# Eight heads' expert weights: added on GpSimd and transposed once, in place of four accumulating products on TensorE

## The chip, the core and the metric

The kernel runs on one core of a Trainium2 chip. The metric is the device time of one execution in microseconds (us). A core has five instruction queues that run side by side and meet only through semaphores: TensorE (PE in the rows, its weight loads PEld), VectorE (DVE), ScalarE (ACT), GpSimd (POOL) and SyncE (SP), which here only issues transfers.

## What is computed

A layer norm, an attention block with three branches (compressed, selected, windowed), and a feed-forward part that picks experts by product keys; the output is x + attention * silu(feed-forward). The change lies in the feed-forward part:

```python
q = (x @ Wq.T).reshape(b, n, 2, HEADS, DIM_KEY).transpose(2, 0, 1, 3, 4)
sim = jnp.einsum('pbnhd,hkpd->pbnhk', q, keys)
sx, ix = jax.lax.top_k(sim[0], TOPK)          # HEADS = 8, TOPK = 16
sy, iy = jax.lax.top_k(sim[1], TOPK)
all_scores = (sx[..., :, None] + sy[..., None, :]).reshape(b, n, HEADS, TOPK * TOPK)
scores, pk_indices = jax.lax.top_k(all_scores, TOPK)
wd = W_down[pk_indices]
wu = W_up[pk_indices]
h = jnp.einsum('bnd,bnhkd->bnhk', x, wd)
h = jax.nn.gelu(h, approximate=False)
h = h * jax.nn.softmax(scores, axis=-1)
return jnp.einsum('bnhk,bnhkd->bnd', h, wu)
```

The indices are places in the 16x16 grid of rank pairs, the same grid for all heads, and only 50 of its places can be among the first 16. So for each token the kernel needs, for each of these 50 experts, the softmax weight summed over the eight heads. It then multiplies that sum by the gelu of the expert's product and multiplies the result by the matrix of experts.

## The kernel before

The input has 8 batches of 512 tokens, cut into 32 tiles of 128 tokens (TILES; four to a batch, TB). All five programs are written out by hand, as `turn(n)` for n = 0 to 31, with a ring of buffers between them. A tile passes through three to four turns. In turn n:

- TensorE transposes the top ranks of tile n-1 (`top_columns`, L1173), makes the key products of tile n+1 (`scores`, L1164) and the gaps of tile n-1 (`pair_gaps`, L1182). Then it runs the products of the attention that fall on this turn, and `expert_weights(n-3)` (L1197) somewhere among them.
- VectorE finds the top 16 ranks of tile n (`first_8` L858, `strike_8` L869, `next_8` L878); between these it inverts the softmax sums of tile n-3 (`rden`, L848) and does the steps `key`, `slot_key`, `key8` of tile n-2 (L910, L916, L921, L927) and `slot_gap`, `last8` of tile n-1 (L887, L892, L901).
- ScalarE moves results out of PSUM, does the attention's exponentials, and for tile n-2 the softmax's exponentials (`prob`, L626, eight instructions), then `side` (L609) and, at the start of the next turn, `topT` (L594).
- GpSimd runs `weigh(n-3)` (L420: `wgt` = `prob` * `rden`, 128 x 8 x 50), `over` (L402), `drop` (L411), `past` (L393), and by the place of the turn in its batch one or two elementwise steps of the output (`y1` L483, `y3` L490, `y_sb` L496), `actT` (L429), or the scaling of the attention's probabilities (L455 to L465).

`wgt` holds 8 heads x 50 experts for each token. `expert_weights` takes two heads at a time (100 columns) as the stationary operand against the identity and accumulates the four products in PSUM. The result `c_bank` is 100 x 128: transposed, with even heads summed in rows 0 to 49 and odd heads in rows 50 to 99. The two halves are summed later by the matrix of experts, whose rows stand twice. The products are float32, and the trace counts two matmul records for each of them.

Below, "turn 1" means a turn with n = 1 modulo 4, and so on. Between the gaps and the products of the attention TensorE's order differs by turn: in turn 0 the window projections (L1216, L1221) come before `expert_weights`; in turn 1 `expert_weights` comes straight after the gaps and before the products of the selected tokens (L1228 to L1254); in turn 2 straight after the gaps and before the values (L1262 to L1266); in turn 3 after the attention's output (L1281 to L1286) and before the experts' product (L1210). The first batches differ a little: tile 3 does the work of turns 1 and 2 in one.

At the end the last tile's steps run on VectorE (`last_wgt` and on), and GpSimd ends with `weigh(TILES-2)` and `add_input(B-2)`, which writes `y_sb` for the last batch but one. SyncE stores that, and only then VectorE may write the same `y_sb` for the last batch (`last_finish`, L1097, which waits for `y_free`).

## Time and profile before

| | |
|---|---|
| median of 3 runs | 414.4 us (414.19 to 416.38) |
| the profiled execution, its own time | 414.54 us |
| span from its first to its last instruction | 412.7 us |
| TensorE, matmuls | 280.8 us (68%) |
| VectorE | 331.5 us (80%) |
| ScalarE | 236.4 us (57%) |
| GpSimd | 194.2 us (47%) |
| mean granted TensorE clock | 0.83 |

The trace is of one execution. About 1.8 us of its time lie outside its span. A row of the timeline gives the start, the duration, the engine, the line, the operation and what it writes and reads; in square brackets stand the idle time of the engine just before it and what ended it. TensorE rows can be merged (x8). A clock of 1.00 is 2.4 GHz and 0.50 is 1.2 GHz. TensorE durations include an overlap with the next matmul, so starts are a better measure there than ends.

### The profile page before, as it was taken

The page shows a single profiled execution, that of the slowest core. Times are in us where ns is not written, and L with a number is a line of the kernel's source. Part 1 is how long each engine was busy: PE and PEld are TensorE (multiplying, and loading weights), DVE is VectorE, ACT ScalarE, POOL GpSimd, SP SyncE. Part 2 cuts the span into 40 slices and gives each one's busy share as a digit, 9 for nine tenths or more (in the row PEclk, how much of TensorE's full clock was granted, in tenths as well). Part 3 has the DMA queues.
Part 4 walks back from the last instruction along what each step waited for, and adds up shares of the span by engine and source line. Part 5 has one row for each costly group of instructions (what it writes and reads, how often), then busy time and mean ns, then how long its engine had stood idle before and what let it go on. Part 6 is the DMA issues. An engine that isn't in the chain of part 4 may idle for free.

```text
span 412.7 us, 7769 instructions
## 1 busy us (share of the span) xinstructions
PE 280.8 (68%) x1326; PEld 205.9 (50%) x1326; DVE 331.5 (80%) x2923; ACT 236.4 (57%) x1099; POOL 194.2 (47%) x275
## 2 busy tenths in 40 slices
PE   0698804674685777598758875987588759873915
PEld 0533402453564555386536653865366538653704
DVE  5690298959587678998998989989999899899744
ACT  2176601355556485648665856585667565856671
POOL 7650000425243445554555554545555545454561
PEclk9999965698999889758979897689698966896665
DMA  8600000000000000000000000000000000000001
GB/s 199 159 2 2 0 0 1 1 1 2 1 1 2 1 2 2 1 27 1 2 1 18 11 0 2 28 1 1 2 26 2 3 0 26 2 2 0 26 2 51
DMA packets 11113, 6.27 MB, mean 15 GB/s; under 512 B 1332, under 2 KB 10552, under 8 KB 11064
## 3 DMA queue, kind: packets, MB, share of 16 engines
q1 hardware_dynamic: 9736, 5.12, 4.9%
q10 hardware_dynamic: 1328, 0.66, 0.8%
q14 instruction: 38, 0.31, 0.2%
q8 instruction: 11, 0.18, 0.2%
HBM read 3.68 MB, written 2.10 MB: 14 GB/s over the span
## 4 chain that ended last, share of the span: by engine, by line
issue 36%; POOL 32%; PE 14%; DVE 7%; ACT 6%; DMA 3%; POOLq 1%; ACTq 0%; DVEq 0%; SPq 0%
POOL over L402 5%; POOL past L393 5%; POOL wgt L420 5%; POOL drop L411 5%; DMA fwq_sb<-in_L_ffn_Wq 3%; POOL y L490 2%; PE sim L1164 2%; POOL y L483 2%; POOL y_sb L496 2%; POOL rstd L474 2%; POOL p_win L461 1%; DVE sel_m L946 1%; PE s_bank L1150 1%; ACT xn_all L549 1%; PE c_bank L1197 1%
## 5 line engine op out<-in xcount | busy, mean ns | idle before, releaser
L869 DVE MATCH_REPLACE8 rest<-top,sim 128x32 f32<-128x32 f32 x512 | 86.4, 182 | 0.1
L626 ACT ACTIVATE prob<-drop 128x50 f32<-128x50 f32 x248 | 56.7, 237 | 17.2 <-POOL drop L411 17.2
L402 POOL TENSOR_TENSOR over<-key 128x400 bf16<-128x400 bf16 x31 | 26.6, 859 | 81.2 <-DVE key L927 81.2
L411 POOL TENSOR_TENSOR drop<-gap,out_by 128x400 f32<-128x400 f32 x31 | 32.1, 1037 | 48.8 <-ACT out_by L616 48.8
L878 DVE MAX8 top<-rest 128x8 f32<-128x32 f32 x512 | 53.6, 186 | 0.0
L858 DVE MAX8 top<-sim 128x8 f32<-128x32 f32 x496 | 51.2, 195 | 0.0
L1182 PEld LDWEIGHTS t_bank<-gaps_of,topT 128*128 128x128 f32 x128 | 26.4, 231 | 47.9 <-ACT topT L594 46.5
L1182 PE MATMUL t_bank<-gaps_of,topT 128*128 128x200 f32 x128 | 36.3, 416 | 18.5 <-ACT topT L594 18.3
L626 ACT ACTIVATION_READ_ACCUMULATOR prob<-drop 128x1 f32 x248 | 48.0, 193 | 0.0
L1164 PE MATMUL sim<-sim_w,xT_all 128*128 128x512 f32 x64 | 43.5, 768 | 0.8 <-ACT xT_all L563 0.8
L1173 PE MATMUL t_bank<-ident,top 128*128 128x128 f32 x64 | 17.1, 360 | 39.5 <-DVE top L878 38.8
L869 DVE MATCH_VALUE_LOAD rest<-top,sim 128x8 f32 x512 | 42.2, 82 | 0.0
L1197 PE MATMUL c_bank<-ident,wgt 128*100 128x128 f32 x240 | 40.3, 324 | 0.2 <-POOL wgt L420 0.2
L393 POOL TENSOR_TENSOR past<-gap,last 128x400 f32<-128x400 f32 x31 | 27.6, 890 | 26.7 <-DVE last L901 26.7
L1197 PEld LDWEIGHTS c_bank<-ident,wgt 128*100 128x100 f32 x240 | 37.8, 210 | 1.1 <-POOL wgt L420 0.9
L420 POOL TENSOR_TENSOR wgt<-prob,rden 128x400 f32<-128x400 f32 x31 | 27.0, 872 | 19.7 <-DVE rden L848 19.7
L887 DVE TENSOR_TENSOR slot_gap<-t_bank,gap 128x176 f32<-128x176 f32 x32 | 10.7, 335 | 31.8 <-ACT gap L601 31.8
L910 DVE TENSOR_TENSOR key<-side,order 128x400 bf16<-128x400 bf16 x32 | 28.0, 875 | 10.0 <-ACT side L609 10.0
L1173 PEld LDWEIGHTS t_bank<-ident,top 128*128 128x128 f32 x64 | 9.2, 178 | 43.7 <-DVE top L878 41.3
L616 ACT ACTIVATE out_by<-over 128x400 f32<-128x400 bf16 x31 | 16.8, 542 | 17.2 <-POOL over L402 17.2
L927 DVE MAX8 key<-slot_key 128x8 bf16<-128x22 bf16 x256 | 24.1, 169 | 0.1
L901 DVE MAX8 last<-slot_gap 128x8 f32<-128x22 f32 x256 | 24.0, 174 | 0.0
(211 smaller groups left out, 715.4 us busy)
## 6 DMA issues: line engine op xcount, KB each, us to landing
out<-y_sb SPq DMA_DIRECT2D x7, 256.0 KB, 2.3
...
```

What stands on the lines that cost most here:

```text
L393: nc.gpsimd.tensor_tensor(past[:, :, :], gap[n % 3][:, :, :], last8[n % 2][:, :, 7:8].to_broadcast([P, HEADS, CANDS]), ALU.subtract).then_ ...
L402: nc.gpsimd.tensor_tensor(over[:, :, :], key[:, :, :], key8[:, :, 7:8].to_broadcast([P, HEADS, CANDS]), ALU.subtract).then_inc(over_done, 1)
L411: nc.gpsimd.tensor_tensor(drop[:, :, :], gap[n % 3][:, :, :], out_by[:, :, :], ALU.add).then_inc(drop_done, 1)
L420: nc.gpsimd.tensor_tensor(wgt[d][:, :, :], prob[d][:, :, :], rden[d][:, :].unsqueeze(2).to_broadcast([P, HEADS, CANDS]), ALU.mult).then_in ...
L626: last = nc.scalar.activation(prob[d][:, h, :], drop[:, h, :], ACT.Exp, scale=-1.0, accum_out=den[d][:, h:h + 1])
L858: last = nc.vector.max(top[d][:, v, 0:8], sim_bank[d][:, bass.ts(v, KEYS)])
L869: last = nc.vector.match_replace(out=rest[:, v, :], in_to_replace=top[d][:, v, 0:8], in_values=sim_bank[d][:, bass.ts(v, KEYS)], imm_value ...
L878: last = nc.vector.max(top[n % 2][:, v, 8:16], rest[:, v, :])
L910: nc.vector.tensor_tensor(key[:, :, :], side[:, :, :], order[:, :, :], ALU.add).then_inc(key_done, 1)
L1164: mm(sim_bank[n % 2][:, :], xT_all[:, bass.ts(n, P)], sim_w[:, :], start=True, stop=True).then_inc(sim_ready, 1)
L1182: last = mm(t_bank[:, bass.ts(k, HALF_H * CANDS)], topT[:, bass.ts(k, P)], gaps_of[:, :, :].rearrange("p h c -> p (h c)"), start=True, sto ...
L1197: last = mm(o[0:TWO, bass.ts(j, P)], wgt[d][:, h:h + 2, :].rearrange("p h c -> p (h c)"), ident[:, :], start=(h == 0), stop=(h == HEADS - 2))
```

## The change

GpSimd gets two more instructions for each tile, straight behind `wgt`: it adds heads 4 to 7 to heads 0 to 3 (`wgt4`, 128 x 200), and then the upper two of these to the lower two (`wgt2`, 128 x 100). TensorE then transposes `wgt2` once. The two rows of 50 still hold even and odd heads. `wgt4` has one buffer and `wgt2` two. The last tile's adds are done on VectorE, in front of `last_finish`.

```diff
@@ -416,10 +419,24 @@
                 d = n % 2
                 pool.wait_ge(rden_done, n + 1)
                 if n >= 2:
-                    pool.wait_ge(c_ready, n - 1)
+                    pool.wait_ge(wgt4_done, n - 1)
                 nc.gpsimd.tensor_tensor(wgt[d][:, :, :], prob[d][:, :, :],
                                         rden[d][:, :].unsqueeze(2).to_broadcast([P, HEADS, CANDS]),
                                         ALU.mult).then_inc(wgt_done, 1)
+
+            def add_heads(n):
+
+                d = n % 2
+                pool.wait_ge(wgt_done, n + 1)
+                if n >= 1:
+                    pool.wait_ge(wgt2_done, n)
+                nc.gpsimd.tensor_tensor(wgt4[:, :, :], wgt[d][:, 0:HALF_H, :], wgt[d][:, HALF_H:HEADS, :],
+                                        ALU.add).then_inc(wgt4_done, 1)
+                pool.wait_ge(wgt4_done, n + 1)
+                if n >= 2:
+                    pool.wait_ge(c_ready, n - 1)
+                nc.gpsimd.tensor_tensor(wgt2[d][:, :, :], wgt4[:, 0:2, :], wgt4[:, 2:4, :],
+                                        ALU.add).then_inc(wgt2_done, 1)
@@ -500,6 +517,7 @@
                 if n >= 3:
                     weigh(n - 3)
+                    add_heads(n - 3)
@@ -525,12 +543,14 @@
             weigh(TILES - 3)
+            add_heads(TILES - 3)
...
             weigh(TILES - 2)
+            add_heads(TILES - 2)
             add_input(B - 2)
@@ -1102,10 +1122,18 @@
-            dve.wait_ge(c_ready, n - 1)
+            dve.wait_ge(wgt4_done, n - 1)
             nc.vector.tensor_tensor(wgt[d][:, :, :], prob[d][:, :, :],
                                     rden[d][:, :].unsqueeze(2).to_broadcast([P, HEADS, CANDS]),
                                     ALU.mult).then_inc(last_wgt, 1)
+            dve.wait_ge(last_wgt, 1)
+            dve.wait_ge(wgt2_done, n)
+            nc.vector.tensor_tensor(wgt4[:, :, :], wgt[d][:, 0:HALF_H, :], wgt[d][:, HALF_H:HEADS, :],
+                                    ALU.add).then_inc(last_wgt, 1)
+            dve.wait_ge(last_wgt, 2)
+            dve.wait_ge(c_ready, n - 1)
+            nc.vector.tensor_tensor(wgt2[d][:, :, :], wgt4[:, 0:2, :], wgt4[:, 2:4, :],
+                                    ALU.add).then_inc(last_wgt, 1)
             last_finish(0, 0)
@@ -1188,15 +1216,13 @@
                 if n < TILES - 1:
-                    pe.wait_ge(wgt_done, n + 1)
+                    pe.wait_ge(wgt2_done, n + 1)
                 else:
-                    pe.wait_ge(last_wgt, 1)
+                    pe.wait_ge(last_wgt, 3)
                 if n >= TB and n % TB == 0:
                     pe.wait_ge(c_out, n // TB)
-                for h in range(0, HEADS, 2):
-                    last = mm(o[0:TWO, bass.ts(j, P)], wgt[d][:, h:h + 2, :].rearrange("p h c -> p (h c)"),
-                              ident[:, :], start=(h == 0), stop=(h == HEADS - 2))
-                last.then_inc(c_ready, 1)
+                nc.tensor.transpose(o[0:TWO, bass.ts(j, P)],
+                                    wgt2[d][:, :, :].rearrange("p h c -> p (h c)"), ident[:, :]).then_inc(c_ready, 1)
```

TensorE, turns 0 and 1, from the last window projection to the products of the selected tokens; before:

```order
L1221 MATMUL scratch1<-xT_all,wc_sb 128x128 x3
L1197 MATMUL c_bank<-ident,wgt1 100x128 [waits wgt_done]
L1197 MATMUL c_bank<-ident,wgt1 100x128 x3
L1173 MATMUL t_bank<-ident,top0 128x128 [waits slot_gap_done,top_done]
L1173 MATMUL t_bank<-ident,top0 128x128
L1164 MATMUL sim0<-sim_w,xT_all 128x512 [waits sim_used,xt_out]
L1182 MATMUL t_bank<-gaps_of,topT 128x200 [waits topT_out]
L1182 MATMUL t_bank<-gaps_of,topT 128x200
L1197 MATMUL c_bank<-ident,wgt0 100x128 [waits wgt_done]
L1197 MATMUL c_bank<-ident,wgt0 100x128 x3
L1228 MATMUL scratch0<-xn_all,pick 64x128 [waits unit_out,pick_done]
```

The same place after the change:

```order
L1247 MATMUL scratch1<-xT_all,wc_sb 128x128 x3
L1224 MATMUL c_bank<-ident,wgt2_1 100x128 [waits wgt2_done]
L1201 MATMUL t_bank<-ident,top0 128x128 [waits slot_gap_done,top_done]
L1201 MATMUL t_bank<-ident,top0 128x128
L1192 MATMUL sim0<-sim_w,xT_all 128x512 [waits sim_used,xt_out]
L1210 MATMUL t_bank<-gaps_of,topT 128x200 [waits topT_out]
L1210 MATMUL t_bank<-gaps_of,topT 128x200
L1224 MATMUL c_bank<-ident,wgt2_0 100x128 [waits wgt2_done]
L1254 MATMUL scratch0<-xn_all,pick 64x128 [waits unit_out,pick_done]
```

The order is the same; each group of four `c_bank` products is one transpose, and it waits for a later semaphore.

GpSimd, turn 2, before (`y3` is the step in front of `over`):

```order
L483 TENSOR_TENSOR y1<-tanh1_f,half_f 128x512 [waits y_step,f_out]
L420 TENSOR_TENSOR wgt1<-prob1,rden1 128x400 [waits c_ready,rden_done]
L490 TENSOR_TENSOR y3<-y1,s_norm1 128x512 [waits y_done,s_done,y_step]
L402 TENSOR_TENSOR over<-key,key8 128x400 [waits out_by_done,key8_done]
L411 TENSOR_TENSOR drop<-gap2,out_by 128x400 [waits den_done,out_by_done]
```

And after:

```order
L500 TENSOR_TENSOR y1<-tanh1_f,half_f 128x512 [waits y_step,f_out]
L423 TENSOR_TENSOR wgt1<-prob1,rden1 128x400 [waits wgt4_done,rden_done]
L433 TENSOR_TENSOR wgt4<-wgt1 128x200 [waits wgt2_done,wgt_done]
L438 TENSOR_TENSOR wgt2_1<-wgt4 128x100 [waits c_ready,wgt4_done]
L507 TENSOR_TENSOR y3<-y1,s_norm0 128x512 [waits y_done,s_done,y_step]
L405 TENSOR_TENSOR over<-key,key8 128x400 [waits out_by_done,key8_done]
L414 TENSOR_TENSOR drop<-gap0,out_by 128x400 [waits den_done,out_by_done]
```

The two adds stand between `wgt` and `y3`, so `y3` moves back by them.

GpSimd, the end of its program, before:

```order
L472 TENSOR_SCALAR var2<-sq2 128x4 [waits squares2]
L474 TENSOR_TENSOR rstd2<-var2,neg_half 128x4 [waits norm2_step]
L476 TENSOR_TENSOR nmr2<-nmean2,rstd2 128x4 [waits norm2_step]
L420 TENSOR_TENSOR wgt0<-prob0,rden0 128x400 [waits c_ready,rden_done]
L496 TENSOR_TENSOR y_sb<-y3,x_sb 128x512 [waits y_free,y_step]
```

And after:

```order
L491 TENSOR_TENSOR rstd2<-var2,neg_half 128x4 [waits norm2_step]
L493 TENSOR_TENSOR nmr2<-nmean2,rstd2 128x4 [waits norm2_step]
L423 TENSOR_TENSOR wgt0<-prob0,rden0 128x400 [waits wgt4_done,rden_done]
L433 TENSOR_TENSOR wgt4<-wgt0 128x200 [waits wgt2_done,wgt_done]
L438 TENSOR_TENSOR wgt2_0<-wgt4 128x100 [waits c_ready,wgt4_done]
L513 TENSOR_TENSOR y_sb<-y3,x_sb 128x512 [waits y_free,y_step]
```

The last write of `y_sb` on GpSimd stands behind both adds.

## Rows read from the trace of the kernel before

**Rows 1.** The page: busy time of the engines, and TensorE's granted clock in 40 slices.

```profile
PE 280.8 (68%) x1326; PEld 205.9 (50%) x1326; DVE 331.5 (80%) x2923; ACT 236.4 (57%) x1099; POOL 194.2 (47%) x275
...
PEclk9999965698999889758979897689698966896665
```

**Rows 2.** Who waited for whom, 120 to 390 us: total us, times, longest.

```profile
DVE rden L848 <- ACT prob L626: 16.5, 19, 2.7
```

**Rows 3.** The page's group of the accumulating products: busy us, mean ns; idle before.

```profile
L1197 PE MATMUL c_bank<-ident,wgt 128*100 128x128 f32 x240 | 40.3, 324 | 0.2 <-POOL wgt L420 0.2
```

**Rows 4.** GpSimd's groups with shapes kept apart: busy us, mean ns.

```profile
L411 POOL TENSOR_TENSOR drop<-gap,out_by 128x400 f32<-128x400 f32 x31 | 32.1, 1037 | 48.8 <-ACT out_by L616 48.8
...
L463 POOL TENSOR_TENSOR p_cs<-p_cs,rgate 128x128 f32<-128x128 f32 x8 | 3.2, 398 | 0.0
```

**Rows 5.** Timeline, turn 3 into turn 0 and turn 1: TensorE, ScalarE, VectorE.

```profile
264.54 1.60 PE L1197 MATMUL c_bank<-ident,wgt 128*100 128x128 f32 x8
...
266.87 0.38 PE L1173 MATMUL t_bank<-ident,top 128*128 128x128 f32 x2
...
267.29 0.38 ACT L594 ACTIVATE topT<-t_bank 128x256 f32<-128x256 f32 x1 [1.10 <-PE t_bank L1173]
...
276.37 0.20 DVE L848 RECIPROCAL rden<-den 128x8 f32<-128x8 f32 x1 [1.05 <-ACT prob L626]
```

**Rows 6.** Timeline of turn 1: GpSimd's weigh, then TensorE.

```profile
276.66 0.86 POOL L420 TENSOR_TENSOR wgt<-prob,rden 128x400 f32<-128x400 f32 x1 [0.65 <-DVE rden L848]
...
277.87 1.04 PE L1197 MATMUL c_bank<-ident,wgt 128*100 128x128 f32 x8
278.83 1.09 PE L1228 MATMUL scratch<-xn_all,pick 128*64 128x128 f32 x8
```

**Rows 7.** Timeline of turn 2: VectorE, GpSimd, TensorE.

```profile
245.13 0.20 DVE L848 RECIPROCAL rden<-den 128x8 f32<-128x8 f32 x1 [0.97 <-ACT prob L626]
...
255.30 0.20 DVE L848 RECIPROCAL rden<-den 128x8 f32<-128x8 f32 x1 [0.43 <-ACT prob L626]
...
245.41 0.86 POOL L420 TENSOR_TENSOR wgt<-prob,rden 128x400 f32<-128x400 f32 x1 [0.76 <-DVE rden L848]
246.22 1.39 POOL L490 TENSOR_TENSOR y<-y,s_norm 128x512 f32<-128x512 f32 x1
...
247.50 1.04 PE L1262 MATMUL scratch<-wo_sb,vw 128*80 128x128 f32 x8
```

**Rows 8.** VectorE's key and slot_key: durations ns min/median/max.

```profile
L910 DVE TENSOR_TENSOR key<-side,order x32: 319/934/1153, 66.7 to 399.0; 128x400 bf16<-128x400 bf16 x32
...
L916 DVE TENSOR_TENSOR slot_key<-key x32: 228/240/656, 67.6 to 399.4; 128x176 bf16<-128x176 bf16 x32
```

**Rows 9.** The first weights (tile 0) on TensorE, and the rden behind them.

```profile
79.39 2.03 PE L1197 MATMUL c_bank<-ident,wgt 128*100 128x128 f32 x8 [0.25 <-POOL wgt L420]
81.34 1.09 PE L1228 MATMUL scratch<-xn_all,pick 128*64 128x128 f32 x8
...
91.30 0.20 DVE L848 RECIPROCAL rden<-den 128x8 f32<-128x8 f32 x1 [3.03 <-ACT prob L626]
```

**Rows 10.** Stretches: engines' busy us (instructions), then the granted clock.

```profile
77.94:81.36 3.42, 3.17 (x13) 2.37 (x11) 3.42 (x39) 0.50 (x1) 0.86 (x1) 0.50 0.00 0
81.36:84.77 3.41, 2.53 (x16) 1.91 (x15) 3.41 (x38) 0.81 (x3) 0.86 (x1) 1.00 0.01 2
...
255.43:258.85 3.42, 3.10 (x11) 2.29 (x10) 3.20 (x26) 0.78 (x3) 1.22 (x3) 0.50 0.00 0
262.26:265.67 3.41, 3.41 (x18) 3.41 (x18) 3.41 (x39) 2.25 (x18) 2.92 (x3) 0.50 0.00 0
```

**Rows 11.** The end: GpSimd's last two steps, and VectorE's last write of y_sb.

```profile
401.51 1.13 POOL L420 TENSOR_TENSOR wgt<-prob,rden 128x400 f32<-128x400 f32 x1 [1.29 <-DVE rden L848]
402.60 1.26 POOL L496 TENSOR_TENSOR y_sb<-y,x_sb 128x512 f32<-128x512 f32 x1
...
406.31 0.43 DVE L1097 TENSOR_TENSOR y_sb<-y,x_sb 128x256 f32<-128x256 f32 x1 [0.92 <-SPq L332]
```

5 lines of the change are left out of this document (4 added, 1 removed).

## The prediction

> **What bounds the kernel now.** I read the page first. VectorE is the busiest engine with 331.5 us of 412.7, TensorE is busy for 280.8 us and GpSimd for 194.2 [rows 1]. That alone would say that a shorter TensorE part is worth nothing and that GpSimd has room. The list of waits says more: between 120 and 390 us VectorE waits 16.5 us, in 19 waits, for the softmax exponentials of ScalarE, just before `rden` [rows 2]. So the turns are ended in part by a chain that runs around VectorE. ScalarE ends its exponentials, `topT` follows, TensorE makes the gaps and the attention's products, ScalarE takes these out in program order, and only behind them come its next exponentials. The `c_bank` products are links of that chain where they stand in front of something that ScalarE waits for. So I ask turn by turn what TensorE does behind them and when their input is there.
>
> **What is removed.** Each tile has eight matmul records with a mean of 324 ns [rows 3]. By starts they hold TensorE for 278.83 - 277.87 = 0.96 us at a clock of 1.00 [rows 6] and for 81.34 - 79.39 = 1.95 us at 0.50 [rows 9, 10]. One transpose replaces them. Two transposes of 128 columns take 0.38 us together at full clock [rows 5], so one takes 0.2 us at full clock and, by the same doubling, up to 0.4 us at half. The saving is about 0.8 us at full clock and 1.5 us at half, if the input is there.
>
> **What is added.** GpSimd does two adds for each tile. The trace has no such form, so I take the rate from the nearest: `drop`, two full float32 inputs of 400 elements, takes 1.037 us, and a step of 128 elements takes 0.398 us [rows 4]. The slope is 0.639 / 272 = 2.35 ns for an element, and this gives 0.57 us for 200 and 0.33 us for 100 elements. The short step repeats one of its inputs, so the slope is rather too steep; I allow 0.57 to 0.65 and 0.33 to 0.40. Before each add GpSimd waits for its own semaphore. A hop from VectorE to GpSimd took 245.41 - 245.33 = 0.08 us [rows 7], and I take the same. The pair takes 1.06 to 1.21 us behind the end of `wgt`. `key` of VectorE follows `wgt` closely and can hold it up: `y3` takes 1.39 us behind it [rows 7] where the last `y_sb`, of the same size, takes 1.26 [rows 11]. With that, 1.1 to 1.4 us.
>
> **Turns 1 and 2: the wait takes the place of the work.** In turn 1 `wgt` ends at 276.66 + 0.86 = 277.52. TensorE begins the products at 277.87 and the selected tokens' product L1228 at 278.83 [rows 6]. With the change `wgt2` is there at 277.52 + 1.1 to 1.4 = 278.6 to 278.9, and 0.2 us for the transpose gives 278.8 to 279.1 for L1228. That is 0 to 0.3 us later than now; I take 0.2. Turn 2 is the same: `wgt` ends at 246.27, `wgt2` at 247.4 to 247.7, and L1262 starts at 247.6 to 247.9 instead of 247.50 [rows 7]. I take 0.3. Queued behind the waiting transpose are all the attention's products of the turn, and ScalarE waits for these before it gets to its exponentials. VectorE has no cover for it there: it waits already, 0.97 us in front of turn 2's `rden` and 0.43 us in front of turn 3's [rows 7]. There are five such turns 1 and six such turns 2 in the regular part, so 5 x 0.2 + 6 x 0.3 = **+2.8 us**, with bounds of 0 and +4.
>
> **Turn 3 into turn 0: the gain.** Here `wgt` follows turn 3's `rden` at 255.30 [rows 7] and is ready long before its products at 264.54, so nothing waits. The products take 264.54 to about 266 at half clock, then come the experts' product and the transposes of the ranks at 266.87, and ScalarE, idle for 1.10 us, starts `topT` at 267.29 [rows 5]. TensorE saves about 1.2 us before the clock rises, of which the later start of the full clock takes back some 0.3. I take 0.9. It passes through `topT`, the gaps, the window projections and the exponentials to the 1.05 us for which VectorE waits in turn 1 [rows 5]. But it needs the half clock. In batches where the clock is full in turn 3, TensorE has caught up by itself, and ScalarE's own exponentials come last. The clock row dips in pairs of neighbouring slices, 7 and 5, 7 and 6, 6 and 6, 6 and 6, at about 165 to 186, 248 to 268, 330 to 351 and 371 to 392 us [rows 1]: four such batches. 4 x -0.9 = **-3.6 us**; bounds -1.8 and -4.4 (1.10 for each).
>
> **The first tiles.** Tile 0's products stand in front of L1228 too, at half clock, and they start as `wgt` ends, at 79.39. So `wgt2` is there at about 80.5 and L1228 could start at 80.9 instead of 81.34. That is -0.5 us. But the stretch from 77.94 to 81.36 was nearly full of matmuls (3.17 of 3.42 us, 2.03 of them these products), and behind it the clock is 1.00 [rows 9, 10]. With TensorE idle in place of most of them, I expect the clock to be 0.50 in the stretch from 81.36 too. L1228 (1.09 us at full clock) is then some 0.9 us longer and the two products of the selected queries and keys behind it together some 0.6, by the same doubling; that lies on a path on which VectorE waits 3.03 us [rows 9]. Net **+1.0 us**; bounds -0.5 and +2.
>
> **The end.** GpSimd ends with `wgt` at 402.64 and then `y_sb` [rows 11]. The store of `y_sb` must land before VectorE may write its own `y_sb` at 406.31, for which it waits 0.92 us, released by SyncE. The two adds now stand in front of `y_sb`, and nothing covers them: **+1.2 us**; bounds +1.0 and +1.4. The two adds of the last tile on VectorE, each no longer than L1097's 0.43 us for 256 elements, fall into the 0.92 us of that wait and cost nothing.
>
> **Edits that I cost at nothing.** In turns 3 and 0 GpSimd's adds lie in its idle time in front of `over` or `actT`. `wgt` now waits for `wgt4_done` of two tiles before, which comes earlier than `c_ready` did. The transposed sum needs no change behind it.
>
> **VectorE and GpSimd on the same memory.** VectorE's `key` takes 0.32 us at best and 0.93 as a median, beside a `wgt` of 0.86; `slot_key` takes 0.24 as a median and 0.66 at worst, beside `y3` [rows 8]. More steps on GpSimd mean more chances to be caught. `slot_key` starts about 0.8 us behind the end of `wgt` (247.07 is the one in turn 2, where `y3` now runs), near the seam between the two adds, so I expect it to slip in between them for under 0.1 us. In turn 2 `y3` moves back by 1.2 us and catches the next short step instead of this one. By the row that moves a loss of 0.4 us; I count nothing. The Trainium skill ("SBUF — State Buffer", section "SBUF: two separate sides") says that the pair of ports that the two share is an exclusive lock for a whole instruction. By that rule the second step would wait out nearly all of `y3`, some 1.1 us in place of 0.4; the wait in front of turn 3's `rden` would hide most of the difference, and the sum would grow by about 1 us.
>
> **The sum** against the profiled execution's own 414.54 us: 2.8 - 3.6 + 1.0 + 1.2 = +1.4, so 415.9. The median of the runs lies 0.1 lower. I forecast **416.0 us**: no change that can be measured (this kernel's measurement can tell about 0.5%, 2.1 us, from no change). With all bounds at one end it is 0 - 4.4 - 0.5 + 1.0 = -3.9, or at the other 4 - 1.8 + 2 + 1.4 = +5.6: 410.6 to 420.1.
>
> **The rivals.** (1) *TensorE's clock falls where it is now full.* The products that go were also what kept TensorE busy at the end of turn 0. If the clock stays at 0.50 through turn 1, the eight products of L1228 take some 0.9 us more, and the smaller products behind them up to as much again, all on the chain. I take 0.8 to 1.7 us in each of five turns 1, +4 to +8 on top of the sum: 420 to 424, and if only two turns are hit 417.5 to 419. For it: the clock row has tenths below 10 in all but a few slices [rows 1], so it changes state all the time, and the first tiles show how it rises behind these very products [rows 9, 10]. Against it: the key products L1164 move into their place. It decides from one hit turn on, as the forecast lies 0.5 us under the bound. A row bears on this: from 255.43 to 258.85 TensorE was busy 3.10 us, partly with transposes of `p_win`, and the clock was still 0.50 at the end of turn 3 [rows 10]. The Trainium skill ("TensorE: Matmul & The Clock Gate", section "Part 4: PE-mode transpose") says that full clock does not engage for transposes. By that rule the new `c_bank` transposes would not help the clock at all, and this rival would be the likelier one; its time is the one above. (2) *The waits behind the exponentials vanish.* If TensorE arrives earlier in most turns, VectorE no longer waits for ScalarE, `key` gets to the memory before `wgt` and takes 0.32 instead of 0.93 us. The 16.5 us of waits [rows 2] are the limit. Half of them, and 0.6 us in six turns, less the +1.2 and +1.0, give about -9.6: 405; a third of it 411. For it: ScalarE's part is in the chain of every turn. Against it: in turns 1 and 2 the transpose must wait for `wgt2`, by starts that are in the rows. (3) *GpSimd's steps catch VectorE's.* If `slot_key` meets an add in each turn 3 and 0, 13 turns x 0.4 us add 5 us: 421. (4) *The change does not do what it says*: the transpose needs as many passes as a product. Then it takes 0.1 us more a tile; that is inside the range.
>
> **How the numbers follow.** The forecast case has 0.46, rival 1 0.29, rival 2 0.16, rival 3 0.09. Faster by over 0.5%, below 412.3: most of rival 2 (0.14) and the lower edge of the forecast case (0.04), 0.18. Slower by over 0.5%, above 416.5: nearly all of rivals 1 and 3 (0.34) and the upper edge of the forecast case (0.03), 0.37. Same: the rest of the forecast case and the mild ends of the rivals, 0.45. The range leaves out the deep end of rival 2 and the far end of rival 1: 411 to 421. The forecast case's own range is 413 to 418.
>
> **What would show it.** Right: TensorE idle for 0.8 us in front of the `c_bank` transpose in turns 1 and 2, released by GpSimd; L1228 and L1262 at the same distance from `rden` as now, or up to 0.3 us more; in batches with half clock in turn 3 an idle time of ScalarE in front of `topT` of 0.2 us in place of 1.10; the last `y_sb` of GpSimd 1.2 us behind `wgt`; adds of 0.6 and 0.35 us. Wrong: a clock row with more 5s and 6s and long L1228 rows (rival 1), a sum of waits in front of `rden` well under 10 us with a median of `key` near 0.35 (rival 2), or `slot_key` at a median of 0.5 (rival 3).

## The result: 0.9% slower by the comparison, and 415.6 to 427.0 us from run to run

| | before | after |
|---|---|---|
| median of 18 runs | 414.77 us (413.60 to 416.45) | 423.74 us (415.56 to 427.03) |
| ratio of the comparison | 1 | 1.0091 (95% interval 1.0062 to 1.0119) |
| profiled execution, its own time and span | 414.54 us, 412.7 us | 424.72 us, 422.9 us |
| mean granted TensorE clock of that execution | 0.83 | 0.79 |

The ratio leaves out the slow runs of a kernel, those more than 1.5% above its fastest, and here these are twelve of eighteen, the profiled one among them, so that the ratio stands for about 418.5 us where the median is 423.7. In the main the times follow the granted clock. A run with a mean clock of 0.838 took 415.56 us, four with 0.824 and 0.825 took 418.4 to 419.2, one with 0.821 took 421.1, those between 0.787 and 0.803 took 423.1 to 425.0, and one with 0.775 took 427.03. The kernel before spreads over 2.9 us, the changed one over 11.5.

The page of the profiled execution, the busy times and the clock row, answers to [rows 1]:

```profile
PE 265.1 (63%) x1102; PEld 176.9 (42%) x1102; DVE 335.3 (79%) x2925; ACT 236.3 (56%) x1099; POOL 227.9 (54%) x337
...
PEclk9999955585889789798969896988698857695555
```

TensorE lost 15.7 us of work (280.8 to 265.1), and GpSimd got 33.7 more. The clock row has three 5s at 53 to 85 us, and 5s and 6s more closely from 338 us on. The groups of the new steps (engine, line, shape, count | busy us, mean ns | idle before) answer to [rows 3]:

```profile
L433 POOL TENSOR_TENSOR wgt<-wgt 128x200 f32<-128x200 f32 x31 | 18.9, 608 | 2.4
L438 POOL TENSOR_TENSOR wgt<-wgt 128x100 f32<-128x100 f32 x31 | 15.5, 499 | 2.4
...
L1224 PE MATMUL c_bank<-ident,wgt 128*100 128x128 f32 x30 | 10.5, 349 | 14.1 <-POOL wgt L438 14.0
```

The last row is the change in one line: of 40.3 us of products 10.5 are left, and 14.0 us of waiting for GpSimd have come, where there were 0.2. (The names drop buffer numbers, so `wgt` here is `wgt`, `wgt4` and `wgt2`; L433 and L438 are the two adds and L1224 the transpose. `rden` is now L868, the top transposes L1201, the selected tokens' product L1254 and the values' product L1288.)

**Turn 1, timeline**, answers to [rows 6]:

```profile
156.54 0.20 DVE L868 RECIPROCAL rden<-den 128x8 f32<-128x8 f32 x1 [1.07 <-ACT prob L646]
156.82 0.85 POOL L423 TENSOR_TENSOR wgt<-prob,rden 128x400 f32<-128x400 f32 x1 [0.67 <-DVE rden L868]
...
157.75 0.61 POOL L433 TENSOR_TENSOR wgt<-wgt 128x200 f32<-128x200 f32 x1
...
158.44 0.54 POOL L438 TENSOR_TENSOR wgt<-wgt 128x100 f32<-128x100 f32 x1
...
159.03 0.32 PE L1224 MATMUL c_bank<-ident,wgt 128*100 128x128 f32 x1 [0.83 <-POOL wgt L438]
159.28 1.09 PE L1254 MATMUL scratch<-xn_all,pick 128*64 128x128 f32 x8
```

The pair is done 1.31 us behind the end of `wgt` (158.98 - 157.67). TensorE waits 0.83 us and begins L1254 2.74 us behind `rden`, against 2.46 before: 0.28 us later.

**Turn 2, timeline**, an early one and one at 332 us, answer to [rows 7]:

```profile
167.18 0.20 DVE L868 RECIPROCAL rden<-den 128x8 f32<-128x8 f32 x1 [0.93 <-ACT prob L646]
...
169.58 1.26 POOL L507 TENSOR_TENSOR y<-y,s_norm 128x512 f32<-128x512 f32 x1
...
169.67 0.32 PE L1224 MATMUL c_bank<-ident,wgt 128*100 128x128 f32 x1 [0.83 <-POOL wgt L438]
169.82 1.04 PE L1288 MATMUL scratch<-wo_sb,vw 128*80 128x128 f32 x8
...
169.95 0.95 DVE L941 TENSOR_TENSOR slot_key<-slot_key,key 128x40 bf16<-128x40 bf16 x1
...
331.68 0.20 DVE L868 RECIPROCAL rden<-den 128x8 f32<-128x8 f32 x1 [0.97 <-ACT prob L646]
...
334.17 0.32 PE L1224 MATMUL c_bank<-ident,wgt 128*100 128x128 f32 x1 [0.83 <-POOL wgt L438]
334.32 1.79 PE L1288 MATMUL scratch<-wo_sb,vw 128*80 128x128 f32 x8
```

Both turns have the same wait and L1288 2.64 us behind `rden` (2.37 before). But in the second one L1288 takes 1.79 us and not 1.04. Two stretches around it (us, then busy time and count of PE, PEld, DVE, ACT, POOL, then the granted clock) say why:

```profile
324.00:334.40 10.40, 6.91 (x39) 4.81 (x38) 8.56 (x79) 5.94 (x27) 6.23 (x8) 1.00 0.01 2
334.40:354.90 20.50, 15.51 (x58) 12.13 (x57) 17.77 (x157) 10.88 (x57) 13.18 (x18) 0.50 0.01 2
```

The clock falls from 2.4 to 1.2 GHz right behind the wait, where in the early batches it fell only after the values were done, and then stays low for 20.5 us.

**The length of a turn**, worked out as the distance from one `rden` to the next in each trace (from about 170 us on; two values where the trace has two kinds of batch), is the measure for all that follows:

| kernel | turn 1 | turn 2 | turn 3 | turn 0 |
|---|---|---|---|---|
| before | 10.3 | 10.2 | 10.5 | 9.5 or 10.6 |
| after, up to 290 us | 10.6 | 10.45 | 10.5 | 9.5 |
| after, from 290 us | 10.6 or 11.5 | 11.3 to 11.65 | 10.1 to 10.5 | 9.5 or 10.4 |

Up to 290 us a batch has the +0.3 of turn 1 and the +0.3 of turn 2 that the working said, and no turn 0 of 10.6. From there on the clock takes 0.8 to 1.2 us more in five turns: three turns 2, one turn 1 and one turn 0.

That is not the whole of it. Cut at the first `rden`, at the seventh (turn 1, near 155 us) and at the last, the spans divide as follows (us; the kernels of experiments 4, 7 and 11 for later):

| kernel | to the first `rden` | the next six turns | on to the last `rden` | behind it |
|---|---|---|---|---|
| before | 78.2 | 74.2 | 251.4 | 8.9 |
| after | 76.5 | 80.0 | 256.3 | 10.0 |
| 4, wait filled | 78.8 | 74.6 | 250.6 | 10.1 |
| 7, turns 1 and 2 only | 76.8 | 80.2 | 253.5 | 8.4 |
| 11, filled in turns 1 and 2 | 77.7 | 77.2 | 250.6 | 10.0 |

In the profiled execution 5.9 us of the 10.2 are lost in the first six turns behind the first `rden`, 4.9 in the long regular part, 1.1 at the end, and 1.7 are gained in front of the first `rden`, where the change has not yet acted.

### The profile page after: what moved, and what is told of

It is laid out like the page before. It is cut to its first block, busy times and chain, and to the rows that moved or that the text cites. A ratio compares the mean times of both kernels' runs of the same rounds, so it can differ in the third digit from the quotient of the medians.

```text
span 422.9 us, 7446 instructions
## 1 busy us (share of the span) xinstructions
PE 265.1 (63%) x1102; PEld 176.9 (42%) x1102; DVE 335.3 (79%) x2925; ACT 236.3 (56%) x1099; POOL 227.9 (54%) x337
## 4 chain that ended last, share of the span: by engine, by line
POOL 41%; issue 33%; PE 9%; DVE 7%; ACT 4%; DMA 3%; POOLq 1%; ACTq 0%; DVEq 0%; SPq 0%
POOL wgt L423 6%; POOL over L405 6%; POOL past L396 6%; POOL drop L414 5%; POOL wgt L433 4%; POOL wgt L438 3%; DMA fwq_sb<-in_L_ffn_Wq 2%; POOL rstd L491 2%; POOL y L500 2%; POOL y L507 2%; POOL y_sb L513 2%; POOL p_win L478 1%; DVE sel_m L966 1%; PE sim L1192 1%; ACT xn_all L569 1%
## 5 line engine op out<-in xcount | busy, mean ns | idle before, releaser
L1210 PE MATMUL t_bank<-gaps_of,topT 128*128 128x200 f32 x128 | 38.4, 435 | 22.8 <-ACT topT L614 22.5
L1192 PE MATMUL sim<-sim_w,xT_all 128*128 128x512 f32 x64 | 46.9, 825 | 0.8 <-ACT xT_all L583 0.8
L1201 PE MATMUL t_bank<-ident,top 128*128 128x128 f32 x64 | 18.4, 381 | 43.1 <-DVE top L898 42.4
L889 DVE MATCH_VALUE_LOAD rest<-top,sim 128x8 f32 x512 | 39.0, 76 | 0.0
L907 DVE TENSOR_TENSOR slot_gap<-t_bank,gap 128x176 f32<-128x176 f32 x32 | 10.5, 330 | 33.7 <-ACT gap L621 33.3
L930 DVE TENSOR_TENSOR key<-side,order 128x400 bf16<-128x400 bf16 x32 | 26.8, 839 | 9.5 <-ACT side L629 9.3
L1201 PEld LDWEIGHTS t_bank<-ident,top 128*128 128x128 f32 x64 | 8.8, 181 | 50.3 <-DVE top L898 47.8
L868 DVE RECIPROCAL rden<-den 128x8 f32<-128x8 f32 x32 | 6.2, 193 | 20.9 <-ACT prob L646 20.8
L621 ACT ACTIVATE gap<-t_bank 128x400 f32<-128x400 f32 x32 | 16.1, 504 | 9.3 <-PE t_bank L1210 9.1
```

Of the source, the lines that this page charges most:

```text
L889: last = nc.vector.match_replace(out=rest[:, v, :], in_to_replace=top[d][:, v, 0:8], in_values=sim_bank[d][:, bass.ts(v, KEYS)], imm_value ...
L930: nc.vector.tensor_tensor(key[:, :, :], side[:, :, :], order[:, :, :], ALU.add).then_inc(key_done, 1)
L1192: mm(sim_bank[n % 2][:, :], xT_all[:, bass.ts(n, P)], sim_w[:, :], start=True, stop=True).then_inc(sim_ready, 1)
L1201: last = nc.tensor.transpose(t_bank[:, bass.ts(k, P)], top[n % 2][:, bass.ts(k, HALF_V), :].rearrange("p v r -> p (v r)"), ident[:, :])
L1210: last = mm(t_bank[:, bass.ts(k, HALF_H * CANDS)], topT[:, bass.ts(k, P)], gaps_of[:, :, :].rearrange("p h c -> p (h c)"), start=True, sto ...
```

## The experiments

Twelve kernels, each timed beside the kernel before. The candidates were: **A**, the prediction's own sum; **C**, TensorE's clock pays for the change (at first: because work is removed; from experiment 3 on: because TensorE waits idle); **G**, GpSimd's added steps hold up the others. A letter is explained again where it stands for something else. The edits are shown by their main lines.

**1. The adds alone.** GpSimd adds, nobody reads the sums, TensorE does its four products as before.

```diff
                 if n >= 3:
                     weigh(n - 3)
+                    add_heads(n - 3)
```

> The kernel before with GpSimd's two adds put in behind each wgt, and nothing that reads them: TensorE still makes its four products from wgt. Theory C (the removed products lower TensorE's clock, and that is most of the change's loss): the clock stays near the 0.83 of before, the only cost is the end (y_sb 1.1 to 1.2 us later), so 415.5 to 416.5 and a spread between runs as narrow as that of the kernel before. Theory G (the adds themselves cost, on the memory that GpSimd shares with VectorE): 418 to 424, with the step slot_key thirds of VectorE longer in many turns.

Measured: 415.85 us (415.06 to 417.66), ratio 1.0037 (1.0016 to 1.0058). The turns have the lengths of before. What remains is the end: `y_sb` of GpSimd moved back, and VectorE now waits 1.23 us for its store instead of 0.92. Its row:

```profile
407.28 0.43 DVE L1116 TENSOR_TENSOR y_sb<-y,x_sb 128x256 f32<-128x256 f32 x1 [1.23 <-SPq L335]
```

G falls: 34 us more of GpSimd's work cost about 1 us. By the trace that is the end: 10.0 us behind the last `rden`, not 8.9.

**2. The transpose alone.** One transpose of the first two heads of `wgt` in place of the four products, without adds or a new wait.

```diff
-                for h in range(0, HEADS, 2):
-                    last = mm(o[0:TWO, bass.ts(j, P)], wgt[d][:, h:h + 2, :].rearrange("p h c -> p (h c)"),
-                              ident[:, :], start=(h == 0), stop=(h == HEADS - 2))
-                last.then_inc(c_ready, 1)
+                nc.tensor.transpose(o[0:TWO, bass.ts(j, P)],
+                                    wgt[d][:, 0:2, :].rearrange("p h c -> p (h c)"), ident[:, :]).then_inc(c_ready, 1)
```

> The kernel before with one transpose of the first two heads of wgt in place of the four products, no adds; six of eight heads are left out of the sum. TensorE waits for wgt as before. Theory C: each turn loses a link of 0.8 to 1.5 us, but the granted clock falls to about 0.80 and gives most of it back: 410 to 418, and the times of single runs differ by several us and follow the clock. Theory G: with no add and no later wait it is plainly faster, 414.7 less 3.6 (turn 3 into 0) less 11 turns of 0.6: 403 to 406, with a narrow spread.

Measured: 403.98 us (402.17 to 407.08), ratio 0.9747 (0.9713 to 0.9781). Turn 1 takes 9.5 to 9.6 us (one 11.3) and turn 2 9.4. That is the number that G gave, though G had fallen with experiment 1; C in its first form, 410 to 418, missed. The work that goes is worth some 10.5 us if its input is there. Taking it away costs the clock little: 0.808 to 0.827 in the six runs, against 0.823 to 0.844 in the 23 of the kernel before beside them. That leaves the waiting as the place of the loss.

**3. The wait alone.** The adds are made (but for the last tile's), and the four products are kept but wait for `wgt2_done`.

```diff
-                nc.tensor.transpose(o[0:TWO, bass.ts(j, P)],
-                                    wgt2[d][:, :, :].rearrange("p h c -> p (h c)"), ident[:, :]).then_inc(c_ready, 1)
+                for h in range(0, HEADS, 2):
+                    last = mm(o[0:TWO, bass.ts(j, P)], wgt[d][:, h:h + 2, :].rearrange("p h c -> p (h c)"),
+                              ident[:, :], start=(h == 0), stop=(h == HEADS - 2))
+                last.then_inc(c_ready, 1)
```

> The adds on GpSimd as in the change, but TensorE still makes the four products from wgt, only behind the semaphore of the second add. This is the wait alone, without the shorter TensorE part. In turns 1 and 2 (11 of the regular ones, 3 early) each product group starts 0.8 to 0.9 us later. Both theories: 11 to 14 times 0.7 plus 1.2 at the end, 423 to 428. Theory C adds: the clock stays at 0.82 or above and the spread is narrow, under 3 us. Theory G alone cannot say why the changed kernel, which has the same waits but a shorter TensorE part behind them, would be as slow as this one.

Measured: 439.49 us (438.24 to 442.94), ratio 1.0612 (1.0576 to 1.0647), about twice the loss that both theories expected. Turn 1 takes 11.45 us (+1.1), which is the wait; turn 2 takes 12.9 (+2.7), which is more than the wait. Its turn 2, timeline, and the stretch behind the wait:

```profile
255.86 0.20 DVE L867 RECIPROCAL rden<-den 128x8 f32<-128x8 f32 x1 [0.98 <-ACT prob L645]
...
258.35 2.03 PE L1217 MATMUL c_bank<-ident,wgt 128*100 128x128 f32 x8 [0.83 <-POOL wgt L437]
...
260.18 1.79 PE L1282 MATMUL scratch<-wo_sb,vw 128*80 128x128 f32 x8
...
262.87 0.50 ACT L620 ACTIVATE gap<-t_bank 128x400 f32<-128x400 f32 x1
```

```profile
258.30:261.70 3.40, 3.35 (x16) 3.35 (x17) 2.60 (x22) 0.00 (x0) 1.94 (x3) 0.50 0.01 2
```

The wait itself moves the products by 1.0 us (2.49 behind `rden`; before, 246.62 - 245.13 = 1.49). The clock falls at this point in every batch, so the products take 2.03 us instead of 1.04 and the values 1.79 instead of 1.04. ScalarE, with 0.00 us of work in the stretch, waits for both, and VectorE waits for ScalarE. That is the 2.7 us.

**4. The wait filled.** The change with three idle products (identity by identity, into the place that the transpose then overwrites) in front of the wait of turns 1 and 2 and of tile 0. (The wait for `c_out` is moved in front of them; it concerns other tiles.)

```diff
+                if dst is None and (n == 0 or n % TB >= 2):
+                    for k in range(3):
+                        mm(o[0:TWO, bass.ts(j, P)], ident[:, 0:TWO], ident[:, :], start=(k == 0), stop=(k == 2))
                 if n < TILES - 1:
                     pe.wait_ge(wgt2_done, n + 1)
```

> The changed kernel with three idle products (identity by identity, into the place that the transpose then overwrites) put in front of TensorE's wait in turns 1 and 2 and for tile 0. They fill 0.7 us of an 0.8 us idle wait and compute nothing that is used. Theory C: the clock comes back to 0.82 or more, the median falls from 423.7 to 415.5 to 418.5, and the spread shrinks to about 3 us. Theory G: nothing gets faster, 423 to 425.

Measured: 414.53 us (413.46 to 415.87), ratio 0.9992 (0.9969 to 1.0015). More work for TensorE, and the median is 9.2 us under the change's own; by the two ratios, whose intervals are apart, it is 1.0% faster. A turn 2, timeline, and two stretches (columns as above):

```profile
287.30 0.20 DVE L868 RECIPROCAL rden<-den 128x8 f32<-128x8 f32 x1 [0.98 <-ACT prob L646]
...
288.79 0.82 PE L1222 MATMUL c_bank<-ident 128*100 128x128 f32 x6
...
289.79 0.32 PE L1227 MATMUL c_bank<-ident,wgt 128*100 128x128 f32 x1 [0.18 <-POOL wgt L438]
289.94 1.04 PE L1291 MATMUL scratch<-wo_sb,vw 128*80 128x128 f32 x8
```

```profile
317.70:334.80 17.10, 11.42 (x68) 8.48 (x67) 15.16 (x140) 10.89 (x47) 10.05 (x12) 1.00 0.01 2
334.80:341.60 6.80, 4.54 (x12) 2.76 (x13) 6.14 (x56) 3.47 (x23) 5.45 (x10) 0.50 0.01 1
```

The fillers delay nothing: the values' product is again 2.64 us behind `rden`, as in the change. Only the idle time in front is 0.18 and not 0.83 us. The clock is full for 17.1 us and half for 6.8 in this batch, where the change at the same place had 20.5 us at half. Every batch is now alike: 10.65, 10.46, 10.4 and 9.5 us. C is shown: same program, same waits for data, and what differs is that TensorE was kept busy in them.

**5. The transposes late.** The change, but in turns 1 and 2 and for tile 0 the transpose stands behind the attention's products of the turn.

```diff
-                if n >= 3:
+                late = n == 3 or j in (1, 2)
+                if n >= 3 and not late:
                     expert_weights(n - 3)
...
                 if n in VALUES:
                     values_out(VALUES[n])
+                if n >= 3 and late:
+                    expert_weights(n - 3)
```

> The change, but in turns 1 and 2 and for tile 0 TensorE does the transpose behind the attention's products of the turn and not in front of them, so that it has no idle wait for GpSimd's adds there. The adds on GpSimd and the one transpose stay. Theory C (the removal is worth about 10.5 us, and the wait for the second add, with the clock it loses, is what eats it): 404 to 407, since 403.98 is the time with the products gone and no adds, and the end adds 1.2; spread under 3 us; granted clock about 0.83. Theory A (the prediction's own sum): without the two waits +2.8 and without the first tiles' +1.0 the change would gain 3.6 and lose 1.2 at the end: 412 to 413. Theory D (GpSimd's adds collide with VectorE once VectorE no longer waits): 408 to 411, with slot_key at a median above 0.4 us.

Measured: 403.74 us (401.96 to 406.15), ratio 0.9721 (0.9690 to 0.9752). Turn 2, timeline:

```profile
240.46 0.20 DVE L868 RECIPROCAL rden<-den 128x8 f32<-128x8 f32 x1 [0.34 <-ACT prob L646]
...
241.96 1.04 PE L1288 MATMUL scratch<-wo_sb,vw 128*80 128x128 f32 x8
...
242.87 1.26 POOL L507 TENSOR_TENSOR y<-y,s_norm 128x512 f32<-128x512 f32 x1
...
243.23 0.96 DVE L941 TENSOR_TENSOR slot_key<-slot_key,key 128x40 bf16<-128x40 bf16 x1
...
243.51 0.32 PE L1224 MATMUL c_bank<-ident,wgt 128*100 128x128 f32 x1
```

The values now start 1.50 us behind `rden`, and the transpose comes when the sums are long there. D (collisions on VectorE) is not what limits it: L941 takes 0.96 us here too, and still the ratio is that of experiment 2, which had no adds, within the intervals.

**6. Only turns 3 and 0.** The change for the tiles that TensorE takes in turns 3 and 0, four products for all others; the end as before.

```diff
+    ADDED = [n for n in range(1, TILES - 3) if n % TB < 2]
...
+                if n in ADDED:
+                    nc.tensor.transpose(o[0:TWO, bass.ts(j, P)],
+                                        wgt2[ADDED.index(n) % 2][:, :, :].rearrange("p h c -> p (h c)"),
+                                        ident[:, :]).then_inc(c_ready, 1)
+                    return
```

> The change only for the tiles whose weights TensorE transposes in turns 3 and 0 (numbers 0 and 1 modulo 4, without tile 0 and the last three), where the weights are there long before: adds and one transpose for these, four products for the others and for the end as before. Theory A (the prediction's term for turn 3 into turn 0, -3.6): 410.5 to 412.5. Theory F (rival 1 as it was written: the products of turn 0 are what keeps the clock up in turn 1, so their removal alone drops it): 416 or more. Theory C (only an idle wait costs the clock): as A or lower, 408 to 412, spread under 3 us.

Measured: 413.78 us (411.89 to 415.08), ratio 0.9963 (0.9944 to 0.9982): a gain of 1.6 us, less than half of the 3.6. Turn 0 takes 9.9 us in every batch, where it took 9.5 or 10.6 in turn. The 10.6 fell, but the 9.5 rose, since turn 3 is now at half clock in all batches. Three in a row:

```profile
212.40:225.90 13.50, 11.73 (x41) 8.97 (x42) 12.25 (x114) 6.92 (x41) 10.54 (x15) 0.50 0.00 1
253.30:266.90 13.60, 11.76 (x41) 9.01 (x42) 12.35 (x115) 6.93 (x41) 10.61 (x15) 0.50 0.00 1
294.30:307.80 13.50, 11.70 (x40) 8.94 (x41) 12.13 (x115) 6.89 (x41) 10.55 (x15) 0.50 0.00 1
```

So a part of F (the products removed are what keeps the clock up) holds as well: without them these turns run at half clock in every batch, though it costs little time here. None of the three forecasts held the number.

**7. Only turns 1 and 2.** The other half of the change; the end as before.

```diff
+    ADDED = [n for n in range(TILES - 3) if n == 0 or n % TB >= 2]
```

> The other half: the change only for tile 0 and the tiles whose weights TensorE transposes in turns 1 and 2 (numbers 2 and 3 modulo 4, without the last three), where it waits for the adds; four products in turns 3 and 0 and for the end. Theory A (+2.8 for the waits and +1.0 for the first tiles): 417.5 to 419.5. Theory C (the idle wait also costs clock, and this is where the whole loss sits): 419 to 426 with a spread over 3 us. Theory G (the products of turns 3 and 0, left in, keep TensorE busy enough, so the clock does not fall): as A, with a spread under 3 us.

Measured: 421.39 us (419.23 to 425.13), ratio 1.0161 (1.0116 to 1.0207). The loss sits here, +6.0 us, and with it much of the spread, as C said. The halves do not add up to the whole by medians: 6.0 - 1.6 and about 1 us for the end are 5.4, and the change loses 9.0. In this trace, too, the first six turns are the larger part: 6.0 us longer than before, and the regular part 2.1.

**8. Filled for tile 0 only.** The fillers of experiment 4 for tile 0 alone.

```diff
+                if dst is None and n == 0:
+                    for k in range(3):
+                        mm(o[0:TWO, bass.ts(j, P)], ident[:, 0:TWO], ident[:, :], start=(k == 0), stop=(k == 2))
```

> The change with three idle products (identity times identity into the place that the transpose then overwrites) in front of the wait for tile 0's weights alone. With them in tile 0 and in all turns 1 and 2 it was 414.53, without any 423.74 on other chips' runs. Theory A (the first tiles' clock is a small term, 1 us or less): 1 us under the change at most, so 417 to 426 with the change's wide spread. Theory C (tile 0's wait carries a large part, the clock of the first turns): 418 to 421. If tile 0 carried all of it: 414.5 to 415.5.

Measured: 420.39 us (415.80 to 427.09), ratio 1.0081 (1.0045 to 1.0118). The spread of 11.3 us is that of the change, and the median 3.4 us below it, which with such a spread is not much of a measurement. So the filler for tile 0 does not by itself hold the clock in the later turns.

**9. The late order with the end of before.** Experiment 5, and the last two tiles by four products.

```diff
+    ADDED = list(range(TILES - 2))
```

> The change with its transposes behind the attention's products in turns 1 and 2 and for tile 0, and with the end as before: the last two tiles go through four products, so nothing stands in front of the last y_sb on GpSimd and VectorE has no adds of its own. Theory C (the end's +1.0 is a term of its own, as the run with unread adds showed): 1.0 us under the run with the late transposes (403.74), 402 to 403.5. Rival (in that run the last wait in front of VectorE's y_sb is 0.53 us, so no more than that is to be had): 403 to 403.7.

Measured: 400.52 us (400.05 to 403.76), ratio 0.9673 (0.9639 to 0.9707). That is 3.2 us under experiment 5 by the medians, more than either theory gave. In the two traces the end accounts for 1.2 us (8.9 us behind the last `rden`, not 10.1). The rest lies in turns that run at another clock in one trace than in the other, and the two intervals overlap. The end's term holds; beyond it this comparison shows nothing.

**10. The products late.** The kernel before with the order of experiment 5, and nothing else: no adds, no transposes of sums.

```diff
-                if n >= 3:
+                late = n == 3 or j in (1, 2)
+                if n >= 3 and not late:
                     expert_weights(n - 3)
...
+                if n >= 3 and late:
+                    expert_weights(n - 3)
```

> The kernel before with one thing changed: in turns 1 and 2 and for tile 0 TensorE does the four accumulating products behind the attention's products of the turn. No adds, no transposes of sums. Theory P (what the late transposes gained was the place in TensorE's order, since the products stood 0.8 us in front of the attention's products in 12 turns and now stand behind all that ScalarE waits for): 404 to 407. Theory Q (the amount of work on TensorE decides, wherever it stands: 0.8 us a tile more than the late transposes, on a path to the ranks' transposes and the key products): 411 to 415. Between: where the products now hold up the next turn's transposes of the ranks, which in turns 2 and 3 are followed by waits of TensorE anyway, 407 to 410.

Measured: 400.76 us (397.76 to 402.42), ratio 0.9663 (0.9628 to 0.9698), better than P's own range. Turn 2, timeline:

```profile
200.53 0.20 DVE L848 RECIPROCAL rden<-den 128x8 f32<-128x8 f32 x1 [0.33 <-ACT prob L626]
...
202.03 1.04 PE L1262 MATMUL scratch<-wo_sb,vw 128*80 128x128 f32 x8
...
203.58 1.12 PE L1197 MATMUL c_bank<-ident,wgt 128*100 128x128 f32 x8
...
203.97 0.50 ACT L601 ACTIVATE gap<-t_bank 128x400 f32<-128x400 f32 x1
```

The values start 1.50 us behind `rden`, not 2.37 [rows 7], and ScalarE is at `gap` while the products still run: it does not wait for them. VectorE waits 0.33 us in front of turn 2's `rden` where it waited 0.97 [rows 7], and not at all in front of turn 3's. With four products a tile this is as fast as experiment 9 with adds and one transpose. It is also the simplest of the kernels near 400 us.

**11. Filled in turns 1 and 2 only.**

```diff
+                if dst is None and n % TB >= 2:
+                    for k in range(3):
+                        mm(o[0:TWO, bass.ts(j, P)], ident[:, 0:TWO], ident[:, :], start=(k == 0), stop=(k == 2))
```

> The change with three idle products in front of the wait in turns 1 and 2 alone, none for tile 0. With fillers in both places it was 414.53 with a spread of 2.4 us, with one for tile 0 alone 420.39 with a spread of 11.3. Theory C (the idle waits of turns 1 and 2 are what lets the clock fall, again and again): 414.5 to 417, spread under 4 us. Theory S (the first turns' clock sets the phase in which all later turns fall; without the filler there the spread stays): 418 to 422, spread over 6 us.

Measured: 417.86 us (417.00 to 419.62), ratio 1.0085 (1.0059 to 1.0110). The median is 5.9 us under the change's and the spread 2.6 us. The ratio does not differ from the change's 1.0091, so the fillers of turns 1 and 2 narrow the spread and bring the median down by that. C is right and S wrong for the spread: it comes from the waits of turns 1 and 2. (C's own range for the time ended at 417.) The batches are as regular as in experiment 4 (10.6, 10.45, 10.5 and 9.5 us). Between this trace and that of experiment 4 there are 1.6 us (3.3 by the medians), all of them in front of 155 us: the first turn behind tile 0's `rden` takes 15.01 us here and 12.57 there, and begins 1.0 us earlier here.

**12. Both.** The late order with four products in turns 1 and 2, adds and one transpose in turns 3 and 0, the end as before.

```diff
+    ADDED = [n for n in range(1, TILES - 3) if n % TB < 2]
...
+                late = n == 3 or j in (1, 2)
```

> The best of both: the accumulation stands behind the attention's products in turns 1 and 2 and for tile 0, as four products without adds; adds and one transpose only for the tiles of turns 3 and 0; the end as before. Theory T (the gain of the turns 3 and 0, 1.6 us alone, adds to the late order, 400.76): 398.5 to 400. Theory U (with the late order nothing waits for those products any more, or the adds collide with VectorE, which now waits less): 400.5 to 402. Theory V (TensorE is idle more and its clock falls more often): 402 or more.

Measured: 400.95 us (399.70 to 401.19), ratio 0.9639 (0.9610 to 0.9669). By median as experiment 10 (400.76), and the intervals of the two ratios overlap. U: in the late order the adds bring nothing that can be told from none.

The lengths of a turn from about 170 us on:

| kernel | turn 1 | turn 2 | turn 3 | turn 0 |
|---|---|---|---|---|
| 3, wait alone | 11.45 | 12.9 | 10.5 | 9.5 |
| 4, wait filled | 10.65 | 10.46 | 10.4 | 9.5 |
| 5, transposes late | 9.2 to 9.65 | 9.15 to 9.76 | 9.6 to 10.5 | 9.5 to 10.9 |
| 6, turns 3 and 0 only | 10.36 | 10.18 | 10.5 | 9.9 |
| 10, products late | 9.2 to 9.65 | 9.4 | 9.6 to 10.4 | 9.5 (one 11.1) |

## Why the prediction was right, and where it was not

The forecast was 416.0 us, no change that can be measured, with 411 to 421. By the ratio the change takes 414.4 x 1.0091 = 418.2 us, inside the range. (The working's own sum, 414.54 + 1.4 less the 0.1 of the median, is 415.8; the forecast stands 0.2 above it.) The likeliest case did not come: the loss of 0.9% lies above the 0.5% that the prediction set as its own bound, in the case of 0.37. And the median over all runs, 423.7, is above the range. That the range held the ratio is in part luck: the sum had no term for the clock in turns 1 and 2 and +1.0 for first tiles whose first turn alone grew by 3.1, while its gain in turn 0 came, but in part for another reason.

- **Turns 1 and 2: right.** +0.28 us and +0.27 us by the rows above, where 0.2 and 0.3 were taken. TensorE sits idle for 0.83 us in front of the transpose, in some turns 1 for 1.06, released by L438 (0.8 was forecast). The adds take 0.608 and 0.499 us on the mean; the second is longer than the 0.33 to 0.40 of the working: it took 0.53 or 0.54 us in 23 of the 31 tiles and 0.40 in the others. The pair behind `wgt`, 1.31 us, is inside 1.1 to 1.4.
- **Turn 3 into turn 0: right in kind, too large by half.** Experiment 6 has this term alone. Its timeline in a batch with half clock in turn 3 answers to [rows 5]:

```profile
267.65 0.39 ACT L619 ACTIVATE topT<-t_bank 128x256 f32<-128x256 f32 x1 [0.43 <-PE t_bank L1198]
...
276.75 0.20 DVE L873 RECIPROCAL rden<-den 128x8 f32<-128x8 f32 x1 [0.24 <-ACT prob L651]
```

  ScalarE is idle in front of `topT` for 0.43 us (1.10 before, 0.2 forecast), VectorE waits 0.24 (1.05 before), and turn 0 takes 9.9 us instead of 10.6: -0.7, where 0.9 was taken. The step that failed is that the term left the batches with full clock in turn 3 at nothing: with fewer products they lose the full clock too, and give 0.4 us back each. So the term is -1.6, not -3.6. In the change itself the 10.6 also goes, down to 9.5, but up to 290 us that is because the clock is full again when turn 3 ends (its transpose there takes 0.28 us), not for the reason given.
- **The first tiles: mechanism right, size wrong.** The term was +1.0, with a bound of +2. Timeline of the first turn behind tile 0's `wgt`, answers to [rows 9]:

```profile
78.84 0.45 PE L1224 MATMUL c_bank<-ident,wgt 128*100 128x128 f32 x1 [1.41 <-POOL wgt L438]
...
79.22 1.97 PE L1254 MATMUL scratch<-xn_all,pick 128*64 128x128 f32 x8
...
82.39 0.98 PE L1261 MATMUL scratch<-csT,wq_sb 128*128 128x192 f32 x2 [0.41 <-ACT csT L656]
...
92.68 0.20 DVE L868 RECIPROCAL rden<-den 128x8 f32<-128x8 f32 x1 [3.03 <-ACT prob L646]
```

  L1254 starts 2.72 us behind `rden` (76.50 us), not 3.14, which is the forecast gain of 0.4, and it takes 1.97 us, which is the forecast 0.9 more. But the working let the clock rise again behind three products. It stayed at 0.50 until 88.7 us, past the attention's scores as well, and the turn came out 3.1 us longer (16.18 against 13.10), and 1.4 us later at its end, since it began 1.7 us earlier. Where TensorE waits idle for tile 0 (this trace and those of experiments 7 and 11) the clock rises again at 88.7, 92.8 and 87.4 us; where the wait is filled (4 and 8) at 78.8 and 79.3, and before at 81.4; in experiment 3, which waits and then makes four products, at 84.2. Not all of the half clock is the wait's, though: the kernel before had full clock from 71.1 to 74.5 us, and this trace did not, ahead of the first wait. Experiment 4 against 11 prices tile 0's filler at 1.6 us by the traces and 3.3 by the medians. The six turns from there together take 5.9 us more than before, and the sum had nothing for the clock in the five behind the first. Some of that may be scatter: experiment 6, with tile 0's products as before, takes 77.0 us for the six, where the kernel before takes 74.2.
- **The end: right.** +1.0 us by the medians of experiment 1 and 1.1 by the traces, where 1.2 was taken. GpSimd's rows and VectorE's last wait, which answer to [rows 11]:

```profile
410.61 1.13 POOL L423 TENSOR_TENSOR wgt<-prob,rden 128x400 f32<-128x400 f32 x1 [1.28 <-DVE rden L868]
...
411.82 0.61 POOL L433 TENSOR_TENSOR wgt<-wgt 128x200 f32<-128x200 f32 x1
...
412.50 0.40 POOL L438 TENSOR_TENSOR wgt<-wgt 128x100 f32<-128x100 f32 x1
...
412.86 1.26 POOL L513 TENSOR_TENSOR y_sb<-y,x_sb 128x512 f32<-128x512 f32 x1
...
416.57 0.42 DVE L1117 TENSOR_TENSOR y_sb<-y,x_sb 128x256 f32<-128x256 f32 x1 [0.53 <-SPq L335]
```

  `y_sb` starts 2.25 us behind the start of `wgt`, against 1.09 before [rows 11].
- **VectorE's short steps: the row was the wrong guide, and it cost nothing.** In turn 2 `y3` moved from the first step of `slot_key` onto the second. The groups (durations in ns, min/median/max) answer to [rows 8]:

```profile
L936 DVE TENSOR_TENSOR slot_key<-key x32: 229/234/536, 65.9 to 408.5; 128x176 bf16<-128x176 bf16 x32
...
L941 DVE TENSOR_TENSOR slot_key<-slot_key,key x32: 183/190/959, 66.8 to 408.8; 128x40 bf16<-128x40 bf16 x32
```

  A step of 40 elements takes 0.95 us beside `y3` instead of 0.19, and ends with it (170.90 and 170.84 in the turn shown). The working took 0.4 us from the row. The Trainium skill ("SBUF — State Buffer", section "SBUF: two separate sides") says that the shared pair is locked for a whole instruction. Here the trace agrees: the step waited 0.76 us, until `y3` ended, where the working by that rule took 1.1. As the working said, the waits behind it hide it: experiment 1 has these steps too, and its turns are as long as before.
- **Rival 1, the clock: its kind came true, its place did not.** It looked for the loss in turn 1, as a consequence of the products missing at the end of turn 0. Up to 290 us turn 0 is as short as it ever was and turn 1 only 0.3 us longer; later one of each is long at half clock, and three turns 2. The fall moved in turn 2, behind the wait for `wgt2`, and that is where L1288 is long. The step of the prediction that failed is the pricing of that wait. It was costed as 0.2 to 0.3 us of later starts; that TensorE is now idle where it was busy was taken into account for tile 0 only, though turns 1 and 2 have the same pattern. By medians the clock in turns 1 and 2, the early ones among them, costs 5.9 us (the change against experiment 11). Whether the transposes as such keep the clock up less than products would, which this rival also named, no run separates: every kernel with transposes also has less work in their place.
- **Rivals 2 and 3: neither came in the change.** VectorE waits 13.6 us in front of `rden` between 120 and 390 us (16.5 before), not under 10; `key` has a median of 0.93 us, as before, and the first step of `slot_key` one of 0.23, not 0.5. The first half of rival 2, the waits that vanish, came in experiment 10: there VectorE waits 7.3 us, and the time is 400.8 us.
- **With the clock kept up, the sum is right.** Experiment 4 is the change without that loss: 414.53 us, ratio 0.9992. The terms +2.8, -3.6 and the end's +1.0 give +0.2 us, and the measured difference is -0.3 us by the ratio. By the traces the regular part is 0.8 us shorter than before, which is 2.8 - 3.6, though the -3.6 is there in the even clock of all batches and not as shorter work at half clock.

What stays open: why the clock's fall comes before the values in some batches and behind them in others of the same trace, and with it why one run takes 415.6 us and another 427.0. The traces show where the fall is, and the fillers show that idle time in front of it matters; no run here fixed by itself where the fall comes. Open too is why the first `rden` came at 76.5 to 79.1 us in the fourteen traces, whatever the kernel.
